# A third unit of every pair turned by VectorE from a second load, and five of eight left to TensorE

## The reference, cut to what matters

```
y       = einsum('bct,bcd->bdt', x, weights[condition])      # rows of y are the tokens
logits  = y @ router_weight.T + router_bias                  # 2048 -> 64 experts
scores  = softmax(logits);  top 8 of them kept
out     = x + y * sum(kept) + kept @ expert_bias
```

## Time and profile before

| | |
|---|---|
| median of 3 runs | 557.86 us |
| the profiled execution, own time | 556.62 us |
| its span | 554.8 us |
| TensorE busy | 541.2 us, 98% of the span |
| VectorE busy | 470.8 us, 85% |
| ScalarE busy | 366.0 us, 66% |
| GpSimd busy | 358.3 us, 65% |
| DMA, share of the 16 engines | 84.6% |
| mean granted TensorE clock | 0.997 |

### The profile page before, as it was taken

One profiled execution on the slowest core, in us unless ns is written; L12 is line 12 of the kernel. 1 busy time (PEld: TensorE's weight loads), 2 busy tenths in 40 slices (PEclk: granted clock), 3 DMA queues, 4 the chain that ended last, 5 costly groups with the idle time before them and its releaser, 6 DMA issues.

```text
span 554.8 us, 12629 instructions
## 1 busy us (share of the span) xinstructions
PE 541.2 (98%) x3360; PEld 476.0 (86%) x3360; DVE 470.8 (85%) x1056; ACT 366.0 (66%) x831; POOL 358.3 (65%) x336
## 2 busy tenths in 40 slices
PE   5889999999999999999999999999999999999997
PEld 4878888888888888888888888888888888888875
DVE  2588889988889898889898888998888998888965
ACT  3467666677666667666667766667767667766661
POOL 0396665776665676665677666677566577566575
PEclk9989999999999999999999999999999999999999
DMA  8987899888899888889888889888889888889336
GB/s 234 310 212 237 301 323 297 268 311 276 300 302 314 266 293 289 294 293 331 270 281 291 300 275 344 274 272 310 273 291 334 285 282 290 275 295 321 151 152 227
DMA packets 61778, 155.96 MB, mean 281 GB/s; under 512 B 5314, under 2 KB 44226, under 8 KB 45634
## 3 DMA queue, kind: packets, MB, share of 16 engines
q1 hardware_dynamic: 61762, 155.77, 84.6%
HBM read 88.64 MB, written 67.11 MB: 281 GB/s over the span
## 4 chain that ended last, share of the span: by engine, by line
PE 91%; DMA 3%; SPq 3%; DVE 1%; issue 1%; ACT 0%; ACTq 0%
PE zt_ps L333 20%; PE xt_ps L321 14%; PE p_ps L389 11%; PE p_ps L381 10%; PE p_ps L383 10%; PE p_ps L382 10%; PE p_ps L390 10%; DMA x_turn<-x 3%; PE scores_ps L356 2%; PE scores_ps L365 1%; PE scores_ps L347 1%; SPq L234 1%; DMA cond_sb<-itok_B 1%; SPq L242 1%; SPq L243 0%
## 5 line engine op out<-in xcount | busy, mean ns | idle before, releaser
L699 POOL TENSOR_TENSOR x_lo<-x_sb,x_hi 128x512 fp32r<-128x512 f32 x256 | 325.0, 1297 | 168.6 <-ACT x_hi L459 168.6
L549 DVE TENSOR_TENSOR xt_lo<-xt_ps,xt_hi 128x512 fp32r<-128x512 f32 x256 | 175.0, 685 | 63.8 <-ACT xt_hi L451 61.3
L451 ACT CAST xt_hi<-xt_ps 128x512 fp32r<-128x512 f32 x256 | 148.3, 583 | 105.5 <-PE xt_ps L321 86.9
L615 DVE SCALAR_TENSOR_TENSOR out_sb<-p_ps,w_sum,x_sb 128x512 f32<-128x512 f32 x256 | 188.9, 738 | 5.7 <-PE p_ps L390 5.6
L459 ACT CAST x_hi<-x_sb 128x1024 fp32r<-128x1024 f32 x128 | 134.2, 1049 | 0.5 <-PE p_ps L390 0.5
L333 PE MATMUL zt_ps<-xt_hi,router_hl 128*128 128x256 f32 x512 | 129.5, 285 | 0.1
L333 PE MATMUL zt_ps<-xt_lo,router_hl 128*128 128x256 f32 x512 | 129.1, 284 | 0.0
L321 PE MATMUL xt_ps<-ident,x_sb 128*128 128x128 f32 x784 | 119.6, 277 | 1.2 <-DMA x_sb<-x 1.1
L381 PE MATMUL p_ps<-x_hi,w_hl 128*128 128x512 f32 x256 | 118.5, 463 | 0.0
L333 PEld LDWEIGHTS zt_ps<-xt_hi,router_hl 128*128 128x128 f32 x512 | 97.9, 191 | 6.9 <-DVE xt_lo L549 0.8
L321 PEld LDWEIGHTS xt_ps<-ident,x_sb 128*128 128x128 f32 x784 | 95.0, 146 | 10.1 <-DMA x_sb<-x 2.0
(11 more groups left out here) (40 smaller groups left out, 371.4 us busy)
## 6 DMA issues: line engine op xcount, KB each, us to landing
out<-out_sb SPq DMA_DIRECT2D x63, 1024.0 KB, 5.0
x_sb<-x SPq DMA_DIRECT2D x62, 1024.0 KB, 7.3
x_turn<-x SPq DMA_DIRECT2D x120, 128.0 KB, 5.7
w_sb<-L_cond_weights SPq DMA_DIRECT2D x64, 64.0 KB, 5.9
x_sb<-x SPq DMA_DIRECT2D x4, 256.0 KB, 5.0
x_sb<-x SPq DMA_DIRECT2D x2, 512.0 KB, 8.5
out_sb<-L_ffn_expert_bias SPq DMA_DIRECT2D x2, 512.0 KB, 12.4
out<-out_sb SPq DMA_DIRECT2D x4, 256.0 KB, 3.4
```

The lines of the kernel that those rows point to most:

```text
L451: act.copy(xt_hi[:, n % 2, :, r, :], xt_ps[v % 4][:, :].rearrange("p (q c) -> p q c", c=P)).then_inc(xt_hi_ready, 1)
L549: dve.tensor_tensor(xt_lo[:, n % 2, :, r, :], xt_ps[v % 4][:, :].rearrange("p (q c) -> p q c", c=P), xt_hi[:, n % 2, :, r, :].bitcast(F32) ...
L615: dve.scalar_tensor_tensor(out_sb[:, r, cols], p_ps[n % 2][:, :], w_sum[:, o % 2, r:r + 1], x_sb[:, (2 * o + r) % XRING, cols], ALU.mult, ...
L699: pool.tensor_tensor(x_lo[:, r, cols], x_sb[:, (2 * o + r) % XRING, cols], x_hi[:, r, cols].bitcast(F32), ALU.subtract).then_inc(x_lo_read ...
```

## The change: what it does

From pair 2 on VectorE turns unit 6 too (r = 0 of piece 3, `THIRD`), from a second load of that piece of the first batch alone (`x_third`, four DMAs of 64 KB, in runs of 512 bytes). TensorE skips unit 6. VectorE does the new relay at the end of slot 4, behind that slot's finish. SyncE issues the load behind the second batch's matrix and ahead of the second store. Unit 7, which TensorE keeps, shares its route with unit 6 and so is read with the stride of four columns, in every pair, as is the router's piece 3 once.

```diff
+THIRD = 3
...
+        def third(m, o, v):
+            return v == 2 * THIRD and not early(m, o)
...
+            def load_third(m, o):
+                i = 4 * m + o
+                wait(sp, relaid_in_ps, 3 * (i - EARLY - 1))
+                for a in range(GROUPS):
+                    t0 = THIRD * PIECE + a * RUN
+                    sp.dma_start(x_third[32 * a:32 * (a + 1), o % 2, :, :],
+                                 x_pairs[i, :, 0:GROUPS, t0:t0 + RUN]).then_inc(x_third_loaded[o % 2], 16)
...
                         load_weights(m, i, r)
                         if r == 0:
                             load_turned(m, i)
+                        else:
+                            load_third(m, i)
                         store(m, i - 3, r)
...
-                if n == TURNED and not early(m, o):
+                if n == TURNED and not early(m, o) or third(m, o, v):
                     return
...
-                    if n == TURNED:
+                    if n in (TURNED, THIRD):
                         block_of_x = x_sb[:, (2 * o + r) % XRING, n * PIECE:(n + 1) * PIECE].rearrange(
                             "c (k j) -> c j k", k=P)[:, q, :]
...
+                source = x_turn[:, o % 2, r, :, :]
...
+                if v == 2 * THIRD:
+                    source = x_third[:, o % 2, :, :]
+                    dve.wait_ge(x_third_loaded[o % 2], 16 * GROUPS * (2 * m + o // 2))
                 wait(dve, xt_lo_ready, SLOTS * i + v - 3)
...
                     if new and (v + 2) // 2 == TURNED and not early(m, i):
                         relay(m, i, v + 2)
+                    if new and third(m, i, v + 2):
+                        relay(m, i, v + 2)
```

More of the change, by code:

```diff
@@ L85, in adaln_router @@
         x_turn = sb("x_turn", [P, 2, 2, GROUPS, RUN])
+        x_third = sb("x_third", [P, 2, GROUPS, RUN])
         x_hi = sb("x_hi", [P, 2, T], F32R)
@@ L128, in adaln_router @@
         x_turn_loaded = [sem(f"x_turn_loaded{i}") for i in range(2)]
+        x_third_loaded = [sem(f"x_third_loaded{i}") for i in range(2)]
         out_stored = [sem(f"out_stored{i}") for i in range(2)]
@@ L230, in load_turned @@
                 i = 4 * m + o
-                wait(sp, relaid_in_ps, 2 * (i - EARLY - 1))
+                wait(sp, relaid_in_ps, 3 * (i - EARLY) - 4)
                 for a in range(GROUPS):
@@ L272, in _ @@
             load_turned(0, 2)
+            load_third(0, 2)
             sp.wait_ge(router_in_ps, 2)
@@ L278, in _ @@
                     load_turned(0, 3)
+                else:
+                    load_third(0, 3)
                 store(0, 0, r)
@@ L397, in turn_router @@
                     t = h * TB // 2 + q
-                    if t // BLOCKS == TURNED:
-                        block_of_router = router_sb[:, TURNED * PIECE:(TURNED + 1) * PIECE].rearrange(
+                    n = t // BLOCKS
+                    if n in (TURNED, THIRD):
+                        block_of_router = router_sb[:, n * PIECE:(n + 1) * PIECE].rearrange(
                             "e (k j) -> e j k", k=P)[:, t % BLOCKS, :]
@@ L446, in xt_high @@
                 elif n == TURNED:
-                    act.wait_ge(relaid_in_ps, 2 * (i - EARLY) + v - 2 * TURNED + 1)
-                else:
-                    act.wait_ge(xt_in_ps, 2 * EARLY + 2 * PLAIN * i + (v if n < TURNED else v - 2) + 1)
+                    act.wait_ge(relaid_in_ps, 3 * (i - EARLY) + v - 2 * TURNED + 1)
+                elif third(m, o, v):
+                    act.wait_ge(relaid_in_ps, 3 * (i - EARLY) + 3)
+                else:
+                    skipped = 0 if n < TURNED else 2 if v < 2 * THIRD else 3
+                    act.wait_ge(xt_in_ps, 3 * EARLY + (SLOTS - 3) * i + v - skipped + 1)
                 wait(act, routed, PIECES * i + n - 1)
@@ L555, in relay @@
                 i = 4 * m + o
+                source = x_turn[:, o % 2, r, :, :]
                 if v == 2 * TURNED:
                     dve.wait_ge(x_turn_loaded[o % 2], 16 * GROUPS * (2 * m + o // 2))
+                if v == 2 * THIRD:
+                    source = x_third[:, o % 2, :, :]
+                    dve.wait_ge(x_third_loaded[o % 2], 16 * GROUPS * (2 * m + o // 2))
                 wait(dve, xt_lo_ready, SLOTS * i + v - 3)
                 dve.transpose(xt_ps[v % 4][:, :].rearrange("p (q g c) -> p q g c", g=GROUPS, c=32),
-                              x_turn[:, o % 2, r, :, :].rearrange("p g (c q) -> p q g c", c=32)
+                              source.rearrange("p g (c q) -> p q g c", c=32)
                               ).then_inc(relaid_in_ps, 1)
```

## The result

The changed kernel takes 554.12 us (median of 8 runs, 552.48 to 555.35) against 558.44 for the kernel before, run beside it (8 runs): a ratio of 0.9913, with a 95% interval of 0.9896 to 0.993. The forecast was 553.8. The profiled execution took 553.98 us with a span of 552.1, 2.6 less than the profiled one of before (556.62).

The account below looks back on a forecast made before the run. TensorE, busy all 16.53 us of a step, was taken as the bound; 0.395 us saved less 0.245 waited leaves 0.15. 28 x 0.15 - 0.15, about 4.1 us, takes 557.86 to 553.8 us, range 550.0 to 558.4.

Parts of the forecast that it names:

- TensorE's own gain: TensorE without unit 6's four transposes, unit 7 read with a stride: 0.395 us less a step, lower end 0.315.
- 0.36 + 0.08: TensorE in slot 6: 0.36 us saved by dropping unit 6's transposes, 0.08 by a shorter product no longer behind them.
- The shift of the chain: VectorE's relay behind slot 4's finish delays unit 5's subtraction, and kept_low behind it, by 0.15 us.
- 0.31 and 0.47: Larger delays of unit 5's subtraction: 0.31 us if the relay hands over at its end, 0.47 with gaps both sides.
- What TensorE waits: In slot 0, in front of L389, TensorE waits 0.245 us for kept_low every step, leaving 0.15 us gained.
- slack 0.30: Before the change, kept_low would let slot 0's fifth matmul start at 315.21; it starts at 315.51, 0.30 us later.
- VectorE as the bound: VectorE's work plus its wait at unit 7 allows steps of 16.22 to 16.30 us, under 16.38, so not the bound.
- The load, ScalarE, SyncE at nothing: The third load's transfer (1.2 us), its SyncE issues (2.16 us) and ScalarE's copy of unit 6 are covered, costing nothing.
- The sum: Over the steps with a relay of unit 6: 28 x 0.15 - 0.15, about 4.1 us, giving 553.8 us.
- TensorE keeping its gain: Rival: something shortens the chain to kept_low, 28 x 0.395 = 11 us go, 546.8 us; chance 0.11 including the ground up to it.
- The one in which nothing is left: Rival: the relay's hand-over costs 1.12 us, shift 0.31, gain gone: 557.9 us (555.7 with shift 0.23); chance 0.19.
- the slower one: Rival: behind slot 4's finish the relay lengthens the chain beyond its slack; with shift 0.47, 562.7 us; chance 0.12.

Follow-up runs that it names:

- experiment 3: The changed kernel with ScalarE's second split of x of the first batch moved from slot 6 to behind the copy of unit 7: 548.24 us, ratio 0.9824.
- experiment 8: The kernel before with piece 3 read by TensorE with the stride of four columns in every pair: 561.49 us, ratio 1.0043.
- experiment 5: The kernel before with one more VectorE turn at the end of slot 4, into an SBUF tile nobody reads: 558.93 us, ratio 1.0005.
- experiment 1: The kernel before with the load of x_third added and VectorE waiting for it in slot 4, nothing turned: 559.01 us, ratio 1.000.
- experiment 2: The changed kernel without the third load, the relay of unit 6 reading x_turn instead (wrong piece): 553.47 us, ratio 0.9905.
- experiment 9: The changed kernel with the relay of unit 6 at the end of slot 3 instead of slot 4: 571.69 us, ratio 1.0205.
- experiment 4: The kernel before with only ScalarE's second split of the first batch moved to the end of slot 7: 559.22 us, ratio 0.9997.
- experiment 6: The kernel before with two more VectorE turns in slot 4, into an SBUF tile nobody reads: 628.94 us, ratio 1.1241.
- experiment 7: The kernel before with two extra VectorE turns in slot 4 and both ScalarE splits of the first batch a slot later: 603.89 us, ratio 1.0801.

## Why the prediction was right

**TensorE's own gain.** Predicted 0.395 us a step. Where the wait is gone (experiment 3) the step is shorter by 0.365. Of its terms the stride was put at 0.045 and measured at 0.05 a unit (experiment 8); the rows of slot 6 give the 0.36 + 0.08 as predicted: from L410 at 304.02 to the transposes of unit 7 at 306.37 experiment 3 takes 2.35 us, the kernel before (309.55 to 312.33) 2.78. The last 0.02 to 0.03 I did not trace. The rows of experiment 3, and below them the one of the kernel before:

```profile
304.02 0.40 PE L410 MATMUL p_ps<-expert_hl,kept_t_lo 128*128 128x512 f32 x1
...
306.37 0.65 PE L341 MATMUL xt_ps<-ident,x_sb 128*128 128x128 f32 x4
```

```profile
312.33 0.60 PE L321 MATMUL xt_ps<-ident,x_sb 128*128 128x128 f32 x4
```

**The shift of the chain.** This is the term that was mis-sized: 0.15 predicted, 0.09 measured (7.43 to 7.52 us). The relay costs 1.02 from its start to the next (1.04 in the earlier trace rows), so unit 5 comes 0.12 later, measured from unit 4. And `keep` is shorter by 0.03: from `xt_low` of unit 5 to the reciprocal it is 0.98, before 1.01, the first `e_kept` lasting 0.19 instead of 0.21. In experiment 5 the shift is 0.08. Both ends that I had kept above it, 0.31 and 0.47, are excluded for this place; the next `xt_low` starts at 310.07, inside the relay's duration (309.05 + 1.11 = 310.16), 0.09 us early, as in the earlier trace rows. Of the section of the Trainium skill that stood behind the 0.31 ("VectorE: DVE Perf Modes", "The DRAIN you can't avoid") the prediction gave only the first half. It goes on that a next operation that is not held starts earlier, and these rows show such a start.

**What TensorE waits.** Predicted 0.245 us in front of L389 (now L409) in every step. The weight load shows 0.33, the matmuls stand for 0.17. By the sum: slack 0.30 less a shift of 0.09 leaves 0.21, and 16.53 - 0.21 = 16.32, the step that is measured; predicted was 16.38. `kept_low` to L410 is 0.80 us, predicted 0.81.

**VectorE as the bound.** Not reached, as predicted: in experiment 3 VectorE is busy for 15.57 of 16.17 us, and TensorE has no wait for it that costs a matmul. The one left there, 0.16 us at the weights of the route of units 4 and 5, hides behind the matmuls (L410 at 305.17, the route's first at 305.40). But the number of the prediction, 16.22 to 16.30 us, was no bound of VectorE: experiment 3 runs at 16.165. The prediction had added the 0.74 us of wait at unit 7 as if they were VectorE's own; they were ScalarE's order, and went away when the split went behind the copy.

**The load, ScalarE, SyncE at nothing.** For the step this is shown (experiments 1 and 2, the rows of ScalarE and SyncE). For the span it is not: see the load that landed late. The profiles of experiments 3 and 9, the other two with both the load and the change, have a longer step of this kind too (by 0.34 and 0.38 us, TensorE standing at the same transposes; in experiment 3 the profile names no releaser); those of the kernel before and of experiments 1, 2 and 5 have none in their steady steps. With and without the load the change has ratios of 0.9913 and 0.9905, with intervals that overlap. So whether the third load makes such a late landing likelier, and what it costs in the median, stays open. One row was misread. The 221 GB/s of the earlier trace rows are not those of `x_turn`: the packets that move from 302 to 303 are of 8 KB, and `x_turn`'s small ones move from 306 to 308, at 274 and 215 GB/s. The 1.2 us of the transfer came out right all the same (1.0 to 1.2 by these two).

**The sum.** 28 steps of 0.21 are 5.9 us, and the two profiles differ by only 2.6. The steps account for it to 0.2 us: the start-up (`kept_low` of the third step at 67.81 instead of 66.39) gave back 1.4, the step of 18.02 another 1.7. The start is no effect that a single profile can price: the first `kept_low` came at 33.0 us in the kernel before, at 34.8 in the changed one and at 33.4 to 36.4 in the nine experiments, with 35.5 in experiment 4, which has neither the third load nor the third relay. So the median, 4.3 us less than before, agrees with the forecast of 4.1 in part because two errors cancel: the steps gained more (5.9 for 4.2), and 1.6 us went outside the steps, where I had put 0.15. That the total came so near is luck; the mechanism and the step are not. What the 1.6 us are in the median I can't say, since only one execution has a profile.

**The rivals.** TensorE keeping its gain (546.8) did not come by itself; experiment 3 made it come, at 548.24. The one in which nothing is left and the slower one needed a shift of 0.30 or more, 0.2 us beyond the measured one. Experiments 6 and 9 show the slower one's mechanism, a chain lengthened by more than its slack, with more work or in another place; that nothing is left no run shows. The sum of the second rival has a slip: a shift of 0.23 leaves 28 x 0.07 - 0.23 = 1.7 us, which is 556.1 and not 555.7. And the prices of both leave out GpSimd: with a shift of 0.31 the second `e_kept`, at 310.72 in the kernel before, would start at 311.03, behind GpSimd's start at 310.98, and by experiment 6 would wait for it (an estimate; no run has this shift).

## What to carry to other kernels

Where the order is written out by hand, price an added operation by the slack of the chain that it falls into, not by the engine's idle sum: here the same relay gained 4.3 us in one slot and lost 13 in the slot before. What the bound engine saves, it keeps only as far as the next chain has slack, so look for other work that stands inside that chain and could stand behind it: one split of 1.04 us, worth nothing before the change, was worth 0.155 us a step after it, against 0.21 for the change itself.

## What was not expected of the hardware

VectorE's small `e_kept` (two inputs in SBUF, 0.19 to 0.22 us) took 0.67 and 1.30 us while GpSimd's `x_lo` (two inputs in SBUF) ran, and 0.22 again once GpSimd started later (experiments 6 and 7); `xt_low`, with one input in PSUM, kept its 0.65 to 0.69 us beside GpSimd. The Trainium skill says this in "SBUF — State Buffer", section "Who interferes with whom": a VectorE instruction with two SBUF inputs contends with a GpSimd instruction that reads SBUF, and contention there is an exclusive lock. These runs agree: each `e_kept` ends with a GpSimd instruction (312.79 with 312.69, 314.02 with 313.95). In the changed kernel the second `e_kept` (310.80, 0.21 us) ends 0.08 us after GpSimd has started (310.93), so the cliff is next to it: from these numbers I estimate that a shift of `keep` against GpSimd by 0.15 us would make it wait for up to the 1.26 us of one GpSimd instruction. No run tests that, and the prediction had not looked at it; that the change stayed in front of the cliff is luck too.
